# A.v folded into the score product, logits and rows from one product, and a new engine order for double copies of h0, xn and x2

## What is computed

```
h = tokens(x) * pos            # 19 products of 128 rows: 64 patches a sample, + class + 32 text tokens
# A: heads of 16, complex weights
q,k,v = xh@wq, xh@wk, xh@wv    ; y = ((q k^T) * decay) v  (real part)
out = (silu(x@w1) * (groupnorm(y)*scale+bias)) @ w2       ; h = h + out
# B: x = layernorm(h)
o = softmax(q k^T/4) v @ Wo + bo ; z = layernorm(x+o)*g+b
# C: choose the expert with the largest logit of z@gate_W+gate_b
out = gelu(z@W1[e]+b1[e]) @ W2[e] + b2[e], times softmax weight, + h
```

## Time and profile before

| what | value |
|---|---|
| median of 3 runs | 1498.33 us (1497.97 to 1501.59) |
| the profiled execution: its own time | 1504.05 us |
| span between first and last instruction | 1502.2 us |
| mean granted TensorE clock | 0.975 |
| busy over the span: PE, PEld, DVE, ACT, POOL | 95%, 69%, 64%, 51%, 27% |

### The profile page before, as it was taken

The page is one execution under the profiler, slowest core; times in us unless marked ns, Lnnn a source line. Parts: engine busy times, 40 slices in busy tenths (PEclk is TensorE's granted clock), DMA queues, the critical chain, the costliest instruction groups (busy, mean ns, idle before and its releaser), DMA issues. The chain is left out here.

```text
span 1502.2 us, 40019 instructions
## 1 busy us (share of the span) xinstructions
PE 1431.3 (95%) x15260; PEld 1029.5 (69%) x15261; DVE 959.9 (64%) x2051; ACT 763.3 (51%) x1645; POOL 411.9 (27%) x268
## 2 busy tenths in 40 slices
PE   6899999999999999999999999999999984699996
PEld 4566666666666666666666666666666653699996
DVE  2466666666666666666666666666666754466664
ACT  2255555555555555555555555555555552355654
POOL 0002222222222222222222222222222224266665
PEclk9899999999999999999999999999999985799999
DMA  8322222222222222222222222222222001333331
GB/s 329 117 68 75 78 79 77 81 80 76 78 81 78 75 81 81 78 75 77 79 80 77 77 83 77 80 76 82 78 76 68 13 15 37 90 102 102 102 100 57
DMA packets 94836, 124.56 MB, mean 83 GB/s; under 512 B 56587, under 2 KB 77117, under 8 KB 94176
## 3 DMA queue, kind: packets, MB, share of 16 engines
q1 hardware_dynamic: 38112, 102.47, 21.3%
q0 software_dynamic: 56576, 19.93, 6.6%
HBM read 101.27 MB, written 20.82 MB: 81 GB/s over the span
## 5 line engine op out<-in xcount | busy, mean ns | idle before, releaser
L332 PE MATMUL bank_emb<-x_sb,wtok 128*128 128x256 f32 (+1 forms) x1216 | 350.8, 398 | 0.0
L964 POOL DMA_INDIRECT expert_rows<-row_sb,placei x128 | 275.7, 2154 | 103.3 <-issue 103.3
L761 DVE TENSOR_TENSOR sm<-bank_s,con 97x776 f32<-97x776 f32 x256 | 235.2, 961 | 98.1 <-PE bank_s L367 98.1
L332 PEld LDWEIGHTS bank_emb<-x_sb,wtok 128*128 128x128 f32 (+1 forms) x1216 | 207.8, 191 | 87.6 <-issue 45.8
L947 POOL COPY h<-txt 128x128 f32<-128x128 f32 x32 | 9.4, 293 | 887.1 <-DVE h L845 869.6
L765 DVE TENSOR_REDUCE mx<-bank_s 97x8 f32<-97x776 f32 x128 | 120.3, 961 | 52.2 <-PE bank_s L404 52.1
L1134 POOL DMA_INDIRECT out_tokens<-yo,tok x104 | 126.6, 1217 | 91.0 <-issue 55.5
L770 DVE TENSOR_TENSOR prob<-bank_s,mx 97x776 f32<-97x776 f32 x128 | 120.3, 961 | 2.2
L367 PE MATMUL bank_s<-qm,xn 32*97 32x388 f32 x1024 | 118.9, 524 | 1.1 <-ACT qm L664 0.5
L645 ACT ACTIVATE prob<-prob 97x776 f32<-97x776 f32 x128 | 107.8, 843 | 20.8 <-DVE prob L770 20.8
L1064 PE MATMUL bank_s<-w2e,hid 128*128 x832 | 109.8, 275 | 0.0
(11 more groups left out here) (185 smaller groups left out, 2573.3 us busy)
## 6 DMA issues: line engine op xcount, KB each, us to landing
x_sb<-in_x_main SPq DMA_DIRECT2D x96, 768.0 KB, 4.4
row<-expert_rows SPq DMA_DIRECT2D x104, 129.0 KB
w1e<-in_exp_w SPq DMA_DIRECT2D x1, 2576.0 KB, 12.3
txt<-in_txt_t SPq DMA_DIRECT2D x32, 64.0 KB, 1.7
w2e<-in_exp_w SPq DMA_DIRECT2D x1, 2048.0 KB, 16.6
expert_rows<-row_sb,placei POOLq DMA_INDIRECT x128, 7.7
out_tokens<-yo,tok POOLq DMA_INDIRECT x104, 2.6
x_sb<-in_x_tail SPq DMA_DIRECT2D x32, 48.0 KB, 3.6
```

Source lines behind the costliest of these rows:

```text
L332: mm = pe.matmul(banks["emb"][:, 0:NPG], wtok[0:k, c, :], x_sb[0:k, c, :], start=(c == 0), stop=(c == KC - 1))
L761: drain(dve.tensor_tensor(sm[:, k % 2, 2 * h:2 * h + 2, :], pair(h), decay, ALU.mult), name)
L964: pool.indirect_dma_start(out=rows[:, :], out_offset=bass.IndirectOffsetOnAxis(ap=placei[:, k, g:g + 1], axis=0), in_=row_sb[:, k, g, :], ...
```

## The change

1. **Values of A in the score product.** qm is laid out by sample, and has 64 more columns behind the 388 of a sample: the folded value weights of the row group. One product of 452 columns gives scores and values. `a_values`, its two bank uses and ScalarE's two copies are gone; VectorE copies the 64 columns of each bank to vp (`a_value_rows`, 97x128 elements, 8 for a group). A bank pair is free when both its decay product and its value copy are done.
2. **Logits and rows in one product.** th (stationary) times gate_rows = [gate_W, identity], 136 columns, four matmuls in two uses C.rows0 and C.rows1; ScalarE copies both to row_sb, two copies of 97x272, and VectorE adds the gate bias from there.
3. **Two copies** of h0, xn and x2 (by parity of the group): `tokens(g)` waits only for A.out of group g-2. The square and the reciprocal root of A's group norm have tiles of their own (sqy, rsy).
4. **The order.** The bodies are lists of steps with a group offset each; C works on group i-3, rank and placing on i-4, and the second half of B (probabilities, sums, mixing) on i-2. The embedding of the next group lies in blocks of up to three. There are 37 rounds (i from -1 to 35) instead of 34 bodies.

```diff
-    ("C.trows", "z"), ("A.scores1.0", "s0 s1"), ("A.scores1.1", "s2 s3"), ("A.y", "x"), ("A.scores2.0", "s0 s1"),
+    ("A.scores0.1", "s2 s3", 0), ("C.rows1", "x", 3), ("C.var2", "y", 2), ("B.scores0.0", "s0 s1", 1),
+FIRST, LAST = -1, NG + 4
...
-        h0 = sb("h0", [P, G, S])
+        h0 = sb("h0", [P, 2, G, S])
-        xn = sb("xn", [P, N])
-        qm = sb("qm", [P, 4, N])
+        xn = sb("xn", [P, 2, N])
+        qm = sb("qm", [P, G, 4 * S + 2 * 32])
-        x2 = sb("x2", [P, N])
+        x2 = sb("x2", [P, 2, N])
...
-                    mm = pe.matmul(bank_s[0:S, g, 0:4 * S], xn[rows32, t], qm[rows32, :, t], start=True, stop=True)
+                    mm = pe.matmul(bank_s[0:S, r, 0:4 * S + 64], xn[rows32, g % 2, t], qm[rows32, k, :],
+                                   start=True, stop=True)
...
-            def a_values(i, half):
-                ps = use(pe, i, f"A.v{half}")
-                for k in range(2):
-                    t = (2 * half + k) * S
-                    mm = pe.matmul(ps[0:S, k * 2 * P:(k + 1) * 2 * P], xn[:, t:t + S], vc[:], start=True, stop=True)
-                done(mm, f"A.v{half}")
...
-            def c_logits(i):
-                pe.wait_ge(s_th, i - 1)
-                ps = use(pe, i, "C.logits")
-                for c in range(4):
-                    mm = pe.matmul(ps[0:S, c * E:(c + 1) * E], th[:, c * S:(c + 1) * S], weight("gate_W"),
-                                   start=True, stop=True)
+            def c_rows(g, half):
+                pe.wait_ge(s_th, g + 1)
+                ps = use(g, f"C.rows{half}")
+                for c in range(2):
+                    t = (2 * half + c) * S
+                    mm = pe.matmul(ps[0:S, c * (E + P):(c + 1) * (E + P)], th[:, t:t + S], gate_rows[:],
+                                   start=True, stop=True)
+                done(mm, f"C.rows{half}")
...
+            def a_decayed(g, k, h, last=False):
+                name = f"A.scores{k}.{h}"
+                full(dve, g, name)
+                if k >= 2:
+                    dve.wait_ge(s_mixed, 3 * g + k - 1)
+                decay = const("decay", S)[:, 8 * h * S:8 * (h + 1) * S].rearrange("p (g t) -> p g t", g=2)
+                ins = dve.tensor_tensor(sm[:, k % 2, 2 * h:2 * h + 2, :], pair(h), decay, ALU.mult)
+                if last:
+                    drain(ins, name)
+
+            def a_value_rows(g, k, h, last=False):
+                name = f"A.scores{k}.{h}"
+                full(dve, g, name)
+                ins = dve.tensor_copy(vp[:, k, 4 * h:4 * h + 4, :, 0:DH].rearrange("p (r m) o e -> p r (m o) e", r=2),
+                                      pair(h, 4 * S, 4 * S + 64).rearrange("p r (q e) -> p r q e", e=DH))
+                if last:
+                    drain(ins, name)
...
             def tokens(g):
                 dve.wait_ge(s_xused[3], g + 1)
+                if g >= 2:
+                    read(dve, g - 2, "A.out")
...
+                at(a_scores, i, 1)
+                at(embed, i + 1, 9, 12)
+                at(a_mix, i, 0)
+                at(a_scores, i, 2)
+                at(a_mix, i, 1)
+                at(b_values, i - 1)
+                at(embed, i + 1, 12, 13)
+                at(a_scores, i, 3)
...
+            for i in range(FIRST, LAST):
+                at(text, i)
+                at(scatter, i - 4)
```

More of the change, by code:

```diff
@@ new lines, in b_values, with b_scores @@
+            def b_values(g):
+                read(pe, g, "B.center")
+                ps = use(g, "B.v")
+                for c in range(4):
+                    mm = pe.matmul(ps[0:S, c * P:(c + 1) * P], x2[:, g % 2, c * S:(c + 1) * S], weight("Wv"),
+                                   start=True, stop=True)
+                done(mm, "B.v")
+            def b_scores(g, k):
+                if k == 0:
+                    read(pe, g, "B.q")
+                    read(pe, g, "B.k")
+                for r in range(4):
+                    name = f"B.scores{k}.{r // 2}"
+                    if r % 2 == 0:
+                        use(g, name)
+                    rows32 = slice(32 * r, 32 * r + 32)
@@ L633, in values, with log @@
[L633 to L643 removed]
+            def log(g, name, dst):
+                ps = full(act, g, name)
+                drain(act.activation(dst, ps[:, 0:N], ACT.Ln, bias=const("eps")), name)
@@ new lines, in rstd, with a_square, a_log, a_rstd @@
+            def rstd(g, name, dst, s):
+                read(act, g, name)
+                act.activation(dst, dst, ACT.Exp, scale=-0.5).then_inc(s, 1)
+            def a_square(g):
+                square(g, "A.center", sqa[:], s_sqa)
+            def a_log(g):
+                log(g, "A.var", rsa[:])
+            def a_rstd(g):
+                rstd(g, "A.var", rsa[:], s_rsa)
+            def y_square(g):
+                square(g, "A.y", sqy[:], s_sqy)
+            def y_log(g):
+                log(g, "A.yvar", rsy[:])
@@ new lines, in y_rstd, with b_square, b_log, b_rstd @@
+            def y_rstd(g):
+                rstd(g, "A.yvar", rsy[:], s_rsy)
+            def b_square(g):
+                square(g, "B.center", sqb[:], s_sqb)
+            def b_log(g):
+                log(g, "B.var", rsb[:])
+            def b_rstd(g):
+                rstd(g, "B.var", rsb[:], s_rsb)
+            def c_square(g):
+                read(act, g, "B.wo")
+                act.activation(sqc[:], z2[:], ACT.Square).then_inc(s_sqc, 1)
+            def c_log(g):
+                log(g, "C.var2", rsc[:])
@@ new lines, in c_rstd, with a_query @@
+            def c_rstd(g):
+                rstd(g, "C.var2", rsc[:], s_rsc)
+            def a_query(g, o, last=False):
+                ps = full(act, g, "A.qr")
+                if g and not last:
+                    for h in range(2):
+                        full(act, g - 1, f"A.scores3.{h}")
+                ins = act.mul(qm[:, :, 2 * o * S:(2 * o + 1) * S], ps[:, 0:N].rearrange("p (c t) -> p c t", c=G),
+                              const("odd" if o else "even"))
+                if last:
+                    drain(ins, "A.qr")
@@ new lines, in y_normal, with y_gated @@
+            def y_normal(g):
+                dve.wait_ge(s_rsy, g + 1)
+                ps = full(dve, g, "A.y")
+                drain(dve.scalar_tensor_tensor(out=yn[:], in0=ps[:, 0:N], scalar=column("gn_scale"),
+                                               in1=rsy[:], op0=ALU.mult, op1=ALU.mult), "A.y")
+            def y_gated(g):
+                read(dve, g, "A.y")
+                read(dve, g, "A.gate")
+                dve.scalar_tensor_tensor(out=yn[:], in0=yn[:], scalar=column("gn_bias"), in1=gate[:],
+                                         op0=ALU.add, op1=ALU.mult).then_inc(s_yn, 1)
@@ new lines, in place_all, with run_on @@
+            def place_all(g):
+                ps = full(dve, g, "C.rank")
+                if g:
+                    read(dve, g - 1, "C.rank")
+                dve.tensor_tensor(place[:], by_expert(ps[0:S, 0:G * E]),
+                                  run[0:S, :].unsqueeze(1).to_broadcast([S, G, E]), ALU.add).then_inc(s_route, 1)
+            def run_on(g):
+                ps = full(dve, g, "C.rank")
+                routed(g, "place_all")
+                drain(dve.tensor_tensor(run[:], run[:], ps[:, G * E:(G + 1) * E], ALU.add), "C.rank")
```

926 lines of the change are left out of this document (467 added, 459 removed), and 16 rows, old and new, of the table USES.

## The result

The changed kernel takes 1484.12 us (median; 1482.45 to 1486.12), the kernel before, run beside it, 1499.96 us (1497.97 to 1504.47). The ratio is 0.9891, with a 95% interval of [0.9861, 0.992]: faster by 1.1%, where 2.7% was forecast. The time lies just above the upper end of the range (1484). The medians differ by 15.8 us.

The account below looks back on a forecast made before the run. TensorE's throughput was taken to bound the steady part. 29 steps x 1.5 us, start 5 and C 0.5 gave -49, tail +9, together -40: from median 1498.33 to 1458 us; own range 1440 to 1476, 8 in 10 1436 to 1484.

Parts of the forecast that it names:

- the stalls at the boundary: Chained products between two groups: stalls counted down by 0.3 us, and up by 0.1 at A.yvar, per step.
- the tail: B.center of group 30 to the scatter of group 31, 79.7 us before: +9 us, since the new order is deeper.
- the start: B.center of group 0 to group 1, 40.0 us before: some 35 to 36 us in the new order; together -5.
- Columns: TensorE per group: a_values -1.81, c_logits and c_trows -1.12, c_rows +0.91, wider scores +0.43; sum -1.59 us.
- The waits in the loop: Score product, decay and value copies, next score product: waits of 0.1 and 0.2 us ahead of A's third and fourth.
- up to the last B.wo: First part of the tail: about the same length, +1 us, as B's first scores of the last group wait.
- the bank loop binds: Second rival, chance 0.15: value copies and C's small VectorE steps hold score banks longer; step 36.9, 1481 us.
- waits vanish too: First rival, chance 0.12: boundary stalls go and none comes in the loop; step 35.1, 1429 us.
- the third rival: "Slower", chance 0.06: value copies cost as much as 0.5 us each, lengthening the loop's round trip; step 38.3, 1522 us.
- What takes columns off TensorE should come back in full, as long as no new wait appears: Steady part: TensorE throughput bounds it; taking away only a wait has half a microsecond to win.

## Why the prediction was wrong in size

The direction held, and so did the mechanism in the score stretch: the TensorE columns come off, and the waits there are those computed. Three terms of the sum were wrong: the stalls at the boundary, the tail and the start. Point by point:

- **Columns.** A.v -1.81 as said; scores +0.40 for 0.43; `c_rows` 1.00 for 0.91, within the bounds of 0.86 and 1.02. The value copy lasts 0.281 us, close to t_t, and leaving the copies out gave 0.33 us a step. The waits in the loop were put at 0.3 and came out as 0.31 (0.15 at a mixing, 0.16 at an embedding matmul). The 0.04 by which logits and rows gained more in the old order (0.21 for 0.17 by its slots) is within the reading.
- **The step that failed in the steady part** is "I count the boundary stalls down by 0.3, and up by 0.1 at A.yvar". They went up: the 13 products of 388 columns have 0.22 more than before, and transposes and summed heads 0.04. Where the forecast had -0.2, the rows have +0.26. The 0.22 is at one place that the forecast did not name: the product ahead of B.k has 0.79 (686.23) and B.k 0.73 (687.01), where before both had 0.65; the other eleven are as long in sum as before. B.k waits for x2, which VectorE writes from 686.32 to 686.87 (timeline of DVE), behind the residual that B.wo feeds:

```profile
685.78 0.62 DVE L922 SCALAR_TENSOR_TENSOR z<-bank_s,bo,x 128x388 f32<-128x388 f32 x1 [0.62 <-PE bank_s L349]
686.32 0.55 DVE L839 TENSOR_TENSOR x<-bank_y,rsb 128x388 f32<-128x388 f32 x1
```

  In sum, the stalls that were to go are still there. The variance product of Y waits 0.17 at the end of the slot of `b_hrows`, and it, A.out, B.center and B.k have 0.73 to 0.76 for 0.65: their records in the timeline are 0.92 or 0.89 us long where those without a wait have 0.81 to 0.82, so a product that waited is itself 0.1 longer. A transpose between two chained products doesn't cover the way over VectorE or ScalarE; an embedding matmul does, as the two runs that put one there show (0.75 to 0.65, 0.69 to 0.52).
- **Not counted at all**: A's mixings stand singly in the new order, and a single one takes 0.81 where two in a row take 1.48 in the old order (x64 records, 714.31 to 715.79 in the old order without copies); that is 0.14 a step. The embeddings, apart from the 0.16 of wait, are 0.24 shorter, which was not forecast either; that it makes up for half of the boundary's miss is luck. In all the step was 36.47, not 36.1: 11 us of the 21.6 by which the sum was off. The tail has 5.9 of it, the start 3.8, and what follows the first scatter of group 31 has 0.8.
- **The tail**, +14.9 for +9, is the second term that was mis-sized (5.9 us). The timeline of DVE for group 31, B's divided heads and the row numbers:

```profile
1225.46 0.56 DVE L916 TENSOR_TENSOR o<-bank_s,rden 128x388 f32<-128x388 f32 x1 [7.93 <-PE bank_s L519]
...
1241.49 0.45 DVE L1013 CAST placei<-placef 97x4 int32<-97x4 f32 x1
```

  From B.center of group 30 to the first of these it takes 72.9 us; before, the same instruction (L842) began at 1254.42, after 67.7: +5.2, where "up to the last B.wo" was put at +1. From there to the row numbers 16.0 for 10.6: +5.4. Before, the row numbers of group 30 were ready at 1249.65, ahead of this; now the ranks of both groups follow it (those of group 30 end at 1234.49). From row numbers to the first scatter 5.7 for 1.3: +4.4, the queue on POOL. The forecast had nearly all of it in the last two (+8.1, measured 9.8); what it missed is the chain of B, in which each stage of the last groups stands later in its round. The clock fell further as well, 0.58 for 0.79 in the same 41 us, with PE busy in 13 us of them. That taking group 29 out of the queue gains nothing is shown; which link of B's chain costs the 5 us was not tried. That the depth of the new order is what lengthens the tail the other runs bear out: the stretch took 77.9 to 84.5 us in the five kernels in the old order and 91.7 to 95.7 in the nine in the new one.
- **The start**, -1.2 for -5. The second round was to take 35 to 36 us and took 38.06. Its first chain runs at half clock (timeline of PE; and the windows before, after and with the copies on ScalarE, clock in the last column but two):

```profile
59.89 1.66 PE L349 MATMUL bank_s<-sqa,con 128*128 128x388 f32 x2 [0.58 <-ACT sqa L648]
63.47 1.64 PE L349 MATMUL bank_s<-sqb,con 128*128 128x388 f32 x2 [1.92 <-DVE xn L834]
```

```profile
57.00:68.00 11.00, 10.69 (x33) 5.74 (x32) 3.56 (x7) 4.85 (x9) 0.00 (x0) 0.77 0.02 6
```

```profile
57.00:68.00 11.00, 8.50 (x14) 3.75 (x15) 2.42 (x5) 3.48 (x7) 0.29 (x1) 0.53 0.07 26
```

```profile
57.00:68.00 11.00, 8.50 (x27) 3.98 (x26) 4.25 (x7) 5.12 (x10) 0.29 (x1) 0.84 0.01 3
```

  In the old order 33 matmul records lie in these 11 us at a clock of 0.77, in the new one 14 at 0.53: the transposes, sums and mixings of B that stand between the chained products in full rounds don't exist yet, and the products run at 1.2 GHz, 1.66 us for 0.92. B.var, put behind A's chain, waits 1.92 us for its bank, which xn must leave. The clock is a large part of the miss: with the copies on ScalarE it was 0.84 in the same window, and the second round took 35.44 us, inside the forecast's 35 to 36. With setup and tail edited, where this round has the same work as in the changed kernel, it was 0.69, and the round took 37.40. How much of the 2.6 us is the clock's and how much the copies' was not taken apart.
- **Rivals.** The second, "the bank loop binds", named the right sign (waits for "DVE sm" ahead of scores) and a time of 1481 us near the measured one, but not the right place: these waits were 0.3 a step, as in the main forecast, and leaving out the copies brought 11 us, 9.6 of it in the steps (the small steps of C were not tried apart). Its time came near by luck, through the tail and the start. The first, "waits vanish too", failed: no step came under 36.10. The third needed copies of 0.4 us; the copy has 0.28. In the old order, though, the folding is slower, in part for the reason that the third rival gives, the round trip through VectorE.
- The opening sentence, "What takes columns off TensorE should come back in full, as long as no new wait appears", carried its own exception. In the old order 1.41 us of columns came off and the step grew by 0.29; the removed products were the cover. A new wait at the boundary was what the forecast of the new order missed too.
- The Trainium skill (TensorEngine Tiling (Array Packing), PSUM Bottleneck), weighed with the third rival, advises to share the copies out of PSUM between ScalarE and VectorE. Here the trace agrees: on VectorE they cost 0.33 us a step, on ScalarE nothing that shows, and the versions with that are the fastest: 1472.69 us and a ratio of 0.9813, where the changed kernel has 0.9891.

## What to carry to other kernels

When a matmul is removed from a stream that looks full, ask first what it stood between: if another engine must read a bank before the next product may write it, the removed columns come back as a wait, and the saving appears only when other work is put in the same place. Test a fold and the order around it as a table of four, since either alone can read as no gain or a loss. And count the tail by the link at which the last group is late, not by the queue that looks busiest.

## What the runs showed of the hardware

- ScalarE copied 97x128 elements out of a PSUM bank in 0.24 to 0.27 us, VectorE in 0.281. The two worked side by side on different banks without slowing VectorE: a pair of decay products took 1.84 us, as in the earlier trace rows.
- A product of 388 columns that had waited for its operand took 0.1 us more after the wait than one that had not (slot 0.75 for 0.65), and an embedding matmul put ahead of it took both the wait and this away. Its like without a wait, the variance product of C behind a rows product, has 0.65 (689.97 in the changed kernel).
- Two mixings of A in a row took 1.48 us, two apart 0.81 each.
